# Gathers of edge rows without a wait between them, one wait at the end of each pass

## The chip, the cores and the metric

The kernel runs on one core of a Trainium2 chip. TensorE (PE, its weight loads PEld), VectorE (DVE), ScalarE (ACT), GpSimd (POOL) and SyncE (SP) each run their own instruction stream and meet at semaphores; DMAs are issued by SP and POOL (a few by ACT) and run on 16 DMA engines. The metric is the device time of one execution in microseconds, the median of several.

## The reference

A graph of 50000 nodes with 128 float32 features each and 25000 edges sorted by their target passes through four networks, one after the other; after each one the input is added and a layer norm follows. The first, a graph attention network of four layers, is the one that the change touches:

```
def _gat_layer(x, src, dst, ea, W, We, a_s, a_d, a_e, b, g, beta):
    h = x @ W
    e = ea @ We
    alpha = h @ a_s
    alpha = alpha[src] + (h @ a_d)[dst] + e @ a_e
    alpha = leaky_relu(alpha); alpha = _segment_softmax(alpha, dst, N)
    out = segment_sum(h[src] * alpha[:, None], dst) + b
    return layer_norm(out) * g + beta
...
for l in range(L):                      # L = 4, self loops added to the edges
    x = _gat_layer(x, src_f, dst_f, ea_f, W[l], ...)
```

`h[src]`, one row of 128 features and its attention term for every edge, is what the changed lines fetch. The other three networks (a relation network, a graph convolution, a convolution with edge weights) are outside the change.

## The kernel before, in words

The edges are laid out in K = 196 columns of 128: edge p of column c sits in partition p. The nodes are worked in 98 blocks of 512 rows. Nodes without an edge into them ("plain") need no neighbours, so the kernel works them through the layers on their own; nodes with edges live in "slots".

The attention network is a chain of passes. Each is a `Pass` whose five instruction streams start together and meet at its end in a barrier (L76); then POOL clears the pass's semaphores and a second barrier (L79) lets the next pass start. For each layer l there are three: p0 to p3 bring the edges' rows of layer l into the SBUF tile `H` (128 partitions x 196 columns x 136 floats) and do other work beside it; `soft(l)` computes the attention weights from `H`; `slots(l)` sums the weighted rows and writes layer l + 1's table.

What runs beside the gathers differs. In p0 it is `PlainLayers`: all 98 blocks of plain nodes go through the first layers, loaded and stored by SP, with TensorE, ScalarE and VectorE in a written order; at the end of its loop DVE and PE compute the logit terms (`Logits`, 1027 to 1036 us of the profile). In p0 POOL first gathers 196 columns of target rows (L2406) for the slots, which SP stores, and only then the source rows. In p1 to p3, `plain_rows` runs `Plain`: 32 or 33 blocks each of the plain nodes' way through the second and third networks; per block SP issues two loads, the stores of `n0`, of three tables of rows (L2667) and of `z` (L2672). At its end SP waits until all of these have landed (L1599).

The gathers are `gather_rows`, called by `FirstRows.gpsimd` (p0) and `Rows.gpsimd` (p1 to p3). POOL issues one indirect DMA a column (L2358): 128 rows, 544 bytes each in p0 and 528 after it, picked by an index tile, each with the semaphore `got[c % RING]`, RING = 16. Every 16 columns POOL waits until all 16 semaphores have reached the count of the rounds so far (L2355 to L2357), and after the last column for all of them once more (L2360, L2361). In p0 there is another wait before column 164, since `H`'s last 32 columns first hold the slot rows that SP stores. No instruction of the pass reads the source rows; the first to do so is `soft(l)`.

Gathers in other passes have no such ring: L1695 (`rel_rows`, `n_rows`) and L1909 (`sage_rows`) wait only until a buffer of four columns, of which there are four, has been consumed.

Of the kernel before, what the change touches and what calls it, by code (L numbers as in the profile page):

```python
# [32 lines left out]
RING = 16  # L33
# [2314 lines left out]
def gather_rows(kn, pool, got, table, index, rows, width, before=()):  # L2348

    K, bound = kn.K, pool.to_reg(rows - 1)  # L2350
    for c in range(K):
        if c == K - 8 * KT:
            for s, n in before:
                pool.wait_ge(s, n)
        if c and c % RING == 0:  # L2355
            for j in range(RING):
                pool.wait_ge(got[j], c // RING * 16)  # L2357
        pool.indirect_dma_start(kn.H[:, c, 0:width], None, table, bass.IndirectOffsetOnAxis(index[:, c:c + 1], 0),  # L2358
                                bounds_check=bound, oob_is_err=False).then_inc(got[c % RING], 16)
    for j in range(RING):  # L2360
        pool.wait_ge(got[j], len(range(j, K, RING)) * 16)  # L2361


class FirstRows(Stream):
# [31 lines left out]
    def gpsimd(self, pool):  # L2396
        kn = self.kn
        last_row = pool.to_reg(kn.NP - 1)
        for g in range(kn.KG):
            if g >= 4:  # L2400
                pool.wait_ge(self.dput[g % 4], g // 4 * 16)
                pool.wait_ge(self.heads_kept, g - 3)
                pool.wait_ge(self.attr_kept, g - 3)
            for k in range(KT):
                c = g * KT + k
                pool.indirect_dma_start(self.dg[:, g % 4, k, :], None, kn.t0w, bass.IndirectOffsetOnAxis(kn.dst_i[:, c:c + 1], 0),  # L2406
                                        bounds_check=last_row, oob_is_err=False).then_inc(self.dgot[g % 4], 16)
        gather_rows(kn, pool, self.got, kn.t0w.rearrange("n (q w) -> (n q) w", q=2), kn.src2_i, 2 * kn.NP, T0W, self.ends())
# [17 lines left out]
class Rows(Stream):  # L2426
# [11 lines left out]
    def gpsimd(self, pool):  # L2438
        kn = self.kn
        gather_rows(kn, pool, self.got, kn.tab[self.l], kn.idx, kn.NP + kn.ND, TW)  # L2440
# [671 lines left out]
```

## Time and profile before

| what | value |
|---|---|
| timed runs | 5356.57, 5367.84, 5373.27 us; median 5367.84 |
| profiled execution, first to last instruction | 5398.9 us |
| busy PE, PEld, DVE, ACT, POOL | 71%, 58%, 70%, 59%, 54% |
| p0, first gather of L2358 to the next pass | 772.7 to 1085.9 us |
| p1 | 1281.4 to 1597.6 us |
| p2 | 1793.3 to 2111.1 us |
| p3 | 2305.3 to 2621.1 us |

The page has no other time of the profiled execution than this span. The shares of busy time are means over a chain of passes with different limits, so the passes are read one by one. A wait is put down to the event that came last by the profile; at a barrier that is an engine's sequencer (a name with a q, as POOLq or PEq), and which engine was the late one has to be read from the timeline. DMA share is the busy share of the 16 DMA engines over all queues, summed over packets that may overlap, so it can pass 1. Part 5 of the page and the waits name a group by line and engine; POOL's gathers show as DMA_INDIRECT, their length being the time of the instruction on POOL and not of the transfer.

### The profile page before, as it was taken

The numbers are of one execution on the slowest core, as the hardware profiler recorded it, in microseconds if no ns is written. First come the engines' busy times: TensorE is split into PE (matmuls) and PEld (weight loads), VectorE is DVE, ScalarE is ACT, GpSimd is POOL, SyncE is SP. The second block draws the span as 40 slices with busy tenths as digits, with TensorE's granted clock in tenths as the row PEclk, the third lists the DMA queues.
The fourth block names the chain that finished last, engine by engine and source line by source line (L and its number), as shares of the span: only waits on it lengthen the run. The fifth ranks groups of instructions, "written<-read, shape, count | busy, mean of one in ns | idle before, by whom it ended". The sixth has DMA issues, their size and how long they took to land. (4 is left out here: it accounts for less than half of the span.)

```text
span 5398.9 us, 104328 instructions
## 1 busy us (share of the span) xinstructions
PE 3821.1 (71%) x23663; PEld 3143.4 (58%) x23663; DVE 3792.3 (70%) x10843; ACT 3176.1 (59%) x11279; POOL 2893.9 (54%) x2759
## 2 busy tenths in 40 slices
PE   6355889566747685768575768678688787977775
PEld 5354778565537453645474545456577676866665
DVE  2575889688849784978596767677567675756666
ACT  2022889577848684868482323356577685655554
POOL 0466766603650463066205867676376564757776
PEclk8698999888979797979676767677799998988777
DMA  8898999556955694578463446555489797872221
GB/s 183 129 301 269 383 362 278 176 148 179 283 175 149 203 283 154 156 229 278 149 184 126 131 129 189 167 158 177 165 282 303 248 305 238 246 189 66 62 66 57
DMA packets 918273, 1074.23 MB, mean 199 GB/s; under 512 B 202780, under 2 KB 565066, under 8 KB 917107
## 3 DMA queue, kind: packets, MB, share of 16 engines
q1 hardware_dynamic: 763570, 890.24, 50.5%
q0 software_dynamic: 90944, 180.06, 13.6%
q10 hardware_dynamic: 63556, 1.81, 1.6%
q8 instruction: 56, 0.92, 0.1%
q14 instruction: 147, 1.20, 0.1%
HBM read 509.54 MB, written 566.14 MB: 199 GB/s over the span
## 5 line engine op out<-in xcount | busy, mean ns | idle before, releaser
L2358 POOL DMA_INDIRECT H<-gat_rows,src_i x784 | 804.1, 1026 | 1032.9 <-POOLq L79 620.9
L1909 POOL DMA_INDIRECT s_G<-sage_rows,src_i x588 | 602.4, 1025 | 369.6 <-issue 161.0
L1695 POOL DMA_INDIRECT r_G<-rel_rows,idx x392 | 441.7, 1127 | 216.8 <-issue 110.2
L1708 PE MATMUL r_t<-r_oh,relv 8*128 8x512 f32 x294 | 227.4, 862 | 217.5 <-issue 77.2
L2547 PE MATMUL p_M<-Wg,p_hT 128*128 128x132 f32 x2352 | 336.6, 287 | 63.1 <-DVE p_res L2604 48.8
L1743 ACT ACTIVATE r_mT<-r_t 128x512 f32<-128x512 f32 x147 | 87.4, 594 | 460.4 <-PE r_t L1711 460.1
L2547 PEld LDWEIGHTS p_M<-Wg,p_hT 128*128 128x128 f32 x2352 | 290.3, 192 | 113.0 <-issue 96.0
L2604 DVE SCALAR_TENSOR_TENSOR p_res<-p_M,p_rr,cg 128x132 f32<-128x132 f32 x1176 | 333.8, 346 | 2.5 <-PE p_M L2547 1.4
L1304 PE MATMUL d_S<-ones,d_sqT 128*128 128x1 f32 x1568 | 224.3, 264 | 144.0 <-DVE d_ve L1449 144.0
L2686 PEld LDWEIGHTS p_pl_p<-Wn,p_pl_h 128*128 128x128 f32 x1568 | 205.9, 198 | 201.8 <-ACT p_pl_h L2780 154.9
L2686 PE MATMUL p_pl_p<-Wn,p_pl_h 128*128 128x128 f32 x1568 | 225.3, 289 | 132.6 <-ACT p_pl_h L2780 132.4
L1304 PEld LDWEIGHTS d_S<-ones,d_sqT 128*128 128x128 f32 x1568 | 217.0, 214 | 172.2 <-issue 133.4
L1605 DVE TENSOR_TENSOR_SCAN r_agT<-same_run,r_agT,r_mT 128x512 f32<-128x512 f32 (+1 forms) x144 | 184.4, 1281 | 185.2 <-ACT r_mT L1743 185.1
L1711 PEld LDWEIGHTS r_t<-share_squares,r_G 128*128 128x128 f32 x1176 | 200.8, 258 | 160.5 <-issue 160.5
L963 POOL DMA_INDIRECT gat_rows<-early_mapv,early_mput x196 | 195.1, 995 | 168.8 <-DMA gat_rows<-early_self_map 57.6
L1695 POOL DMA_INDIRECT r_G<-n_rows,src_i x196 | 235.4, 1201 | 78.5 <-issue 54.2
L2119 POOL DMA_INDIRECT share_squares<-features,src_i x196 | 217.1, 1108 | 94.6 <-issue 58.6
L1353 ACT ACTIVATE d_hs<-d_hs,pl 128x128 f32<-128x128 f32 x784 | 248.4, 399 | 15.8 <-DMA d_hs<-gat_rows 11.9
L2406 POOL DMA_INDIRECT H<-gat_rows,dst_i x196 | 196.1, 1001 | 92.9 <-issue 48.9
L1443 DVE TENSOR_TENSOR_SCAN d_yT<-same_run,d_yT,d_T 128x512 f32<-128x512 f32 (+1 forms) x192 | 244.5, 1273 | 0.3 <-ACT d_sqT L1359 0.2
L2111 POOL DMA_INDIRECT out_dram<-tp_v,put_i x196 | 198.7, 1014 | 77.6 <-issue 56.7
L1711 PE MATMUL r_t<-share_squares,r_G 128*128 (+1 forms) x1176 | 236.6, 363 | 0.0
(482 smaller groups left out, 12286.0 us busy)
## 6 DMA issues: line engine op xcount, KB each, us to landing
gat_rows<-p_res SPq DMA_DIRECT2D x294, 264.0 KB
sage_rows<-p_pl_s SPq DMA_DIRECT2D x294, 256.0 KB
gat_rows<-x_row SPq DMA_DIRECT2D x98, 536.0 KB
gat_rows<-d_res SPq DMA_DIRECT2D x147, 264.0 KB
d_hs<-gat_rows SPq DMA_DIRECT2D x147, 256.0 KB
s_hT<-sage_slots_t SPq DMA_DIRECT2D x147, 256.0 KB
slot_rows<-H SPq DMA_DIRECT2D x49, 544.0 KB, 11.5
x_x<-in_x SPq DMA_DIRECT2D x98, 256.0 KB
```

What stands on the lines that cost most here:

```text
L1304: mm = pe.matmul(pS[:, k:k + 1], sqT[:, b.s2, k * P:(k + 1) * P], self.ones[:, :], start=True, stop=True)
L1353: last = act.activation(hs[:, b.s4, k, :], hs[:, b.s4, k, :], ACT.Copy, scale=self.pl[:, bass.ds(b.n * KT + k, 1)])
L1443: v.tensor_tensor_scan(yT[:, b.s4, :], self.same[:, bass.ds(b.n * BLOCK, BLOCK)], pT[b.s2][:, :], 0.0 if first else yT[:, (b.m - 1) % 4, B ...
L1695: pool.indirect_dma_start(self.G[:, g % 4, k, :], None, table, bass.IndirectOffsetOnAxis(index[:, c:c + 1], 0), bounds_check=bound, oob_is ...
L1708: pe.matmul(pt[:, :], kn.relv[:, l, :], self.oh[:, b.m % self.Y, :], start=True, stop=False)
L1711: mm = pe.matmul(pt[:, k * P:(k + 1) * P], self.G[:, b.s4, k, :], share, start=False, stop=(k == KT - 1))
L1909: pool.indirect_dma_start(self.G[:, g % 4, k, :], None, kn.st[self.l], bass.IndirectOffsetOnAxis(kn.idx[:, c:c + 1], 0), bounds_check=boun ...
L2119: pool.indirect_dma_start(self.G[:, c, :], None, kn.f, bass.IndirectOffsetOnAxis(kn.idx[:, c:c + 1], 0), bounds_check=bound, oob_is_err=Fa ...
L2358: pool.indirect_dma_start(kn.H[:, c, 0:width], None, table, bass.IndirectOffsetOnAxis(index[:, c:c + 1], 0), bounds_check=bound, oob_is_er ...
L2547: mm = pe.matmul(self.pM[self.bank(b, j)][:, k // 2, (k % 2) * TW:(k % 2 + 1) * TW], self.hT[l][:, b.s2, k * P:(k + 1) * P], kn.Wg[:, l, : ...
L2604: last = v.scalar_tensor_tensor(self.res[l][:, b.s4, k, :], self.pM[self.bank(b, j)][:, k // 2, (k % 2) * TW:(k % 2 + 1) * TW], self.rr[l] ...
L2686: mm = pe.matmul(bank[:, k * D:(k + 1) * D], xT[:, k * P:(k + 1) * P], w, start=True, stop=True)
```

## The change

The wait inside the loop goes; the one after the loop stays. The semaphores are counted up as before, 12 or 13 gathers to each.

```
--- before.py
+++ after.py
@@ -2352,9 +2352,6 @@
         if c == K - 8 * KT:
             for s, n in before:
                 pool.wait_ge(s, n)
-        if c and c % RING == 0:
-            for j in range(RING):
-                pool.wait_ge(got[j], c // RING * 16)
         pool.indirect_dma_start(kn.H[:, c, 0:width], None, table, bass.IndirectOffsetOnAxis(index[:, c:c + 1], 0),
                                 bounds_check=bound, oob_is_err=False).then_inc(got[c % RING], 16)
     for j in range(RING):
```

## Rows read from the trace of the kernel before

**Rows 1.** Page, part 5: busy us, mean ns, idle us before.

```profile
L2358 POOL DMA_INDIRECT H<-gat_rows,src_i x784 | 804.1, 1026 | 1032.9 <-POOLq L79 620.9
L1909 POOL DMA_INDIRECT s_G<-sage_rows,src_i x588 | 602.4, 1025 | 369.6 <-issue 161.0
L1695 POOL DMA_INDIRECT r_G<-n_rows,src_i x196 | 235.4, 1201 | 78.5 <-issue 54.2
```

**Rows 2.** POOL's waits in p0, p1, p2, p3: total us, times, longest us.

```profile
POOL H L2358 <- DMA H<-gat_rows,src_i: 52.9, 28, 5.5
...
POOL H L2358 <- DMA H<-gat_rows,src_i: 49.2, 27, 4.7
...
POOL H L2358 <- DMA H<-gat_rows,src_i: 50.6, 24, 5.3
...
POOL H L2358 <- DMA H<-gat_rows,src_i: 45.3, 19, 4.9
```

**Rows 3.** SP's waits at the ends of p0 to p3, same columns.

```profile
SPq L76 <- PEq L76: 55.0, 1, 55.0
...
SPq L76 <- PEq L76: 39.6, 1, 39.6
...
SPq L76 <- PEq L76: 32.0, 1, 32.0
...
SPq L76 <- PEq L76: 30.9, 1, 30.9
```

**Rows 4.** DVE's waits, 1000 to 1086 us, same columns.

```profile
DVE soft_pen L1174 <- PEq L79: 49.7, 1, 49.7
```

**Rows 5.** Timeline of p0 and p1: start us, length us, [idle before].

```profile
772.66 1.00 POOL L2358 DMA_INDIRECT H<-gat_rows,src_i  x1 [0.30 <-issue]
...
1069.05 0.99 POOL L2358 DMA_INDIRECT H<-gat_rows,src_i  x1 [2.37 <-DMA H<-gat_rows,src_i]
1070.35 1.00 POOL L2358 DMA_INDIRECT H<-gat_rows,src_i  x1 [0.30 <-issue]
1072.95 1.00 POOL L2358 DMA_INDIRECT H<-gat_rows,src_i  x1 [0.30 <-issue]
1085.92 0.33 SPq L1167 DMA_DIRECT2D same_run<-same_as_before  x1
...
1281.44 1.00 POOL L2358 DMA_INDIRECT H<-gat_rows,src_i  x1 [207.48 <-POOLq L79]
...
1584.92 1.00 POOL L2358 DMA_INDIRECT H<-gat_rows,src_i  x1 [0.30 <-issue]
1597.62 0.33 SPq L1167 DMA_DIRECT2D same_run<-same_as_before  x1
```

**Rows 6.** Windows in p0: length, busy us, then clock, DMA share, GB/s.

```profile
700.00:800.00 100.00, 82.91 (x630) 73.00 (x629) 85.29 (x299) 80.12 (x307) 65.99 (x66) 0.98 1.03 364
800.00:1000.00 200.00, 195.68 (x1559) 176.35 (x1557) 199.58 (x737) 186.89 (x694) 126.90 (x127) 1.00 0.92 281
1050.00:1065.00 15.00, 0.00 (x0) 0.00 (x0) 0.00 (x0) 0.00 (x0) 11.62 (x12) 0.50 0.24 55
```

**Rows 7.** Windows' sums in p1 to p3: 18 bursts, then 21 pauses.

```profile
sum 387.90, PE 315.20 PEld 224.98 DVE 333.36 ACT 326.35 POOL 300.54; mean PE 17.51 PEld 12.50 DVE 18.52 ACT 18.13 POOL 16.70
...
sum 90.80, PE 66.18 PEld 48.87 DVE 72.80 ACT 79.04 POOL 0.39; mean PE 3.15 PEld 2.33 DVE 3.47 ACT 3.76 POOL 0.02
```

**Rows 8.** Windows of L2358 alone, from SP's end in p1, p2, p3.

```profile
1557.00:1586.00 29.00, 19.98 (x20) 0.50 0.20 45
2078.00:2100.00 22.00, 14.95 (x15) 0.50 0.21 46
2589.00:2610.00 21.00, 14.05 (x15) 0.50 0.20 45
```

**Rows 9.** One line's view, L2358: from issue to landing.

```profile
DMA to landing us min/median/max: 2.5/4.0/5.9
```

**Rows 10.** Window of the third sage_rows pass, columns as in rows 6.

```profile
4541.90:4801.40 259.50, 236.87 (x1698) 202.74 (x1699) 176.82 (x399) 161.86 (x481) 200.09 (x196) 0.95 0.76 233
```

More of the change, by code:

```diff
@@ L2354, in gather_rows @@
                 pool.wait_ge(s, n)
-        if c and c % RING == 0:
-            for j in range(RING):
-                pool.wait_ge(got[j], c // RING * 16)
         pool.indirect_dma_start(kn.H[:, c, 0:width], None, table, bass.IndirectOffsetOnAxis(index[:, c:c + 1], 0),
```

## The prediction

> **What bounds the kernel now.** I read the costliest groups of instructions first, because the change touches one line of them. The gathers into `H` (L2358) are 784 instructions, 196 in each of four passes p0 to p3, 1.03 us each; POOL is busy 804 us with them and idle 1033 us before them [rows 1]. Of that idle time 620.9 us lies before the first gather of p1, p2 and p3, while other passes run, and is no loss. The reader should split the rest by what ended it, which the waits of POOL, pass by pass, do: 52.9, 49.2, 50.6 and 45.3 us ended by the landing of these same gathers [rows 2]. That is the ring wait: after 16 issues POOL waits for all 16 semaphores, the one of the gather just issued too, so it drains what is in flight.
>
> POOL's idle time matters only where POOL ends the pass. The barrier waits at the pass ends show that: SP has everything stored and then waits 55.0, 39.6, 32.0 and 30.9 us [rows 3]. The profile puts this down to a "PEq" because all engines meet there; the timeline names the late one. In p0, DVE's last instruction is long over (its next one follows 49.7 us of idle time [rows 4]), while POOL still gathers at 1072.95 and the next stage starts at 1085.92; in p1, 1584.92 and 1597.62 [rows 5]. From the start of POOL's last gather to the next stage it is 12.97 and 12.70 us, the same tail twice. So each of the four passes ends with POOL alone, and what it saves there is saved in the span, until the next engine is the last. The chain that ended last reaches back only into the final pass, so it says nothing here.
>
> **The change part by part.**
>
> Removed: the waits at c = 16, 32, ..., 192, twelve rounds in each pass. A gather that waits for nothing follows the one before by 1.00 us of work and 0.30 us of idle time [rows 5], so each of the counted waits has 0.30 us that stays. What goes is 52.9 - 28 x 0.30 = 44.5 us in p0, 49.2 - 27 x 0.30 = 41.1 in p1, 50.6 - 24 x 0.30 = 43.4 in p2 and 45.3 - 19 x 0.30 = 39.6 in p3 [rows 2]. The 0.30 us before each of the other gathers, put down to "issue", stays.
>
> Left and moved: the final wait for all 16 semaphores and the 12.7 to 13.0 us tail behind the last gather come earlier by the same amount. Nothing on POOL is queued behind the removed waits but the gathers themselves. In p0 the gathers of the last 32 columns still wait for the slot rows' stores; the slot rows were all gathered before the first of these gathers, so that wait has 164 gathers, some 214 us, of room.
>
> Next late. In p0, POOL's tail would begin 44.5 us earlier, so the next stage would start at 1085.92 - 44.5 = 1041.4. DVE was free 49.7 us before its next instruction, that is at 1036.3 [rows 4]; even with some 1.2 us for the barrier it is ready for a start at 1037.5. POOL stays the last by 4 us and p0 saves all 44.5. In p1, SP waited 39.6 us and POOL saves 41.1: SP, with its stores, is now the last, and 39.6 is saved. In p2 SP allows 32.0 of POOL's 43.4, in p3 30.9 of 39.6 [rows 2, 3]. The sum is 44.5 + 39.6 + 32.0 + 30.9 = 147.0 us. Some 20 us of POOL's gain in p1 to p3 (1.5 + 11.4 + 8.7) are worth nothing, because there SP's stores end the pass.
>
> What the denser gathers cost the others. Alone, gathers at the unwaited pace take a DMA share of 0.24 (1050 to 1065 us), and with the layers' transfers the share is 0.92 (800 to 1000) [rows 6]. In that 200 us window POOL ran the gathers at 127/200 of full busy time against 11.62/15 alone [rows 6], so without waits the share would rise by 0.24 x (0.775/0.635 - 1) = 0.05, to 0.97. Before the change the same pace already stands in the trace: within a burst of 16, nothing waits. So the best row for the cost is a comparison of bursts and pauses. In p0, DVE is busy 199.58 of 200 us over bursts and pauses alike [rows 6]: the layers don't notice. In p1 to p3, summed over 18 bursts and 21 pauses, DVE is busy 333.36 of 387.9 us in bursts (86%) and 72.80 of 90.8 in pauses (80%), PE 81% and 73%, ACT 84% and 87% [rows 7]. No engine of the plain rows gets slower while gathers run, so the lower end is 0. The upper end is the DMA time of the gathers that fall into other work now: 20, 15 and 15 of them ran after SP had finished [rows 8], and 50 x 1.305 us x 0.24 share = 15.7 us, if DMA time were all that counted. The nearest row is the burst and pause comparison, which says none; as DVE does wait for the `z` rows' stores in these passes, I take a third, 5 us.
>
> The forecast is 147 - 5 = 142 us: 5398.9 - 142 = 5257 in the profiled execution. The profile gives no other time of that execution than its span, and the timed runs have their median 31 us (0.6%) below it; the removed idle time should be the same in both, so 5367.8 - 142 = 5226 us, 2.6% less.
>
> **Does the queue fill?** The waits also keep at most 16 gathers in flight, so what stands in their place if they go must be priced. A gather landed 2.5 to 5.9 us after its issue, 4.0 in the median [rows 9]; at 1.305 us a gather that is 2 to 5 in flight, far from 16. And the third pass over `sage_rows` (L1909) issues 196 gathers without such a wait: 259.5 us from first to last, 1.33 us each, at a DMA share of 0.76 [rows 10]. p0 to p3 would take 195 x 1.305 = 254 us and a little more.
>
> The Trainium skill speaks against the change at one place: "DMA: Bandwidth & Descriptors", section "Queues, rings and completion order", has each DMA engine take turns between the queues that have work, a packet at a time. By that rule gathers that never pause would take turns from SP's loads and stores all the time, not in 4 of 5 parts of it, and the third rival below would be the outcome; by the bursts of this trace they take the turns already and nobody waits longer. I go by the rows.
>
> **The rivals.**
>
> *Gathers slow down (12%).* Each gather costs more when nothing pauses it. For it: the gathers of `n_rows` (L1695), also without ring waits, took 1201 ns on average [rows 1], 1.50 us with the 0.30. Against it: the bursts' own 1.00 us and rows 10. At 1.50 us a pass would take 195 x 1.50 = 292.5 us. Against the gathers of p0, 300.3 us from first to last, and of p1, 303.5 [rows 5], this saves 7.8 and 11.0; about 11 in p2 and p3 as well. That makes 41 us, POOL still last everywhere: 5327.
>
> *The transfers of p1 to p3 get late by their share (8%).* The 15.7 us are paid in full and the layers of p0 lose as much as a pass does, 5 us. Saved: 147 - 21 = 126, so 5242.
>
> *DMA saturates and the pass itself gets longer: slower than before (3%).* Between 700 and 800 us, with other gathers and their stores, the share was 1.03 and DVE got through 85.29 of 100 us against 99.8 later [rows 6], a factor of 1.17. If gathers without pauses drive the passes there, the 264 us of p0 from the first gather to DVE's end grow by 45 and eat its 44.5; the some 275 to 285 us of p1 to p3 grow by 47 to 48 each and SP's 39.6, 32.0 and 30.9 are overrun by 7, 16 and 17. In sum 40 us more: 5408. It decides from a slowing by 14% in p1 and 11% in p2 and p3; the 0.97 worked out above speaks against it.
>
> *The waits were not what held the gathers (3%).* If the engine stops by itself where the wait stood, for room in its queue, all stays: 5368. Against it: rows 10, where 196 follow one another with no such stop.
>
> **How the numbers follow.** The forecast gets 74%, 5226 with its own range of 5208 to 5245 (147 saved with 12 of luck and the spread of the timed runs, 5357 to 5373, to 125 saved). The range of 8 in 10 goes up past the second rival and partly to the first: 5205 to 5275. A measurement of this kernel tells 0.3% (16 us) from no change; all cases but the last two are faster by more. Faster 0.94, same 0.03, slower 0.03.
>
> **What would show it.** In the changed trace, the waits of POOL on its own gathers should be gone from L2358 but for a few of 0.3 us; 196 gathers should take 254 to 265 us from first to last; SP's wait at the barrier should be near 10 us in p0 (POOL last) and next to nothing in p1 to p3, while POOL arrives there a little early. The start of the stage behind p0 should move to about 1041 us. The forecast is wrong if the mean of a gather grows beyond 1.1 us, if landing takes 10 us or more, or if the last store of SP in p1 comes later than 276 us after its first gather by more than 5 us.

## The result, and the profile after

| | before | changed |
|---|---|---|
| timed runs, median (range) | 5366.06 us (5356.57 to 5373.27) | 5225.52 us (5209.77 to 5228.46) |
| profiled execution | 5398.9 us | 5208.0 us |

Ratio 0.9726, 95% interval 0.9705 to 0.9746: 140.5 us less, faster clear of noise. The forecast was 5226 us.

The costliest groups of the changed kernel, the two that fill `H` (L2355 was L2358, L2403 was L2406), to be read beside [rows 1]:

```profile
L2355 POOL DMA_INDIRECT H<-gat_rows,src_i x784 | 799.4, 1020 | 867.7 <-POOLq L79 629.7
L2403 POOL DMA_INDIRECT H<-gat_rows,dst_i x196 | 195.5, 997 | 91.9 <-issue 58.5
```

The work on POOL is the same, 1.02 us a gather; the idle time before the gathers fell by 165 us, from 1032.9 to 867.7, and of what is left 629.7 is again the time between the passes. What ended the rest: POOL's waits on its own landings, over the whole execution,

```profile
POOL H L2355 <- DMA H<-gat_rows,src_i: 0.9, 3, 0.3
```

and, in p0, p1, p2 and p3, on nothing that the profile shows:

```profile
POOL H L2355 <- issue: 59.1, 194, 0.3
...
POOL H L2355 <- issue: 59.1, 194, 0.3
...
POOL H L2355 <- issue: 59.4, 195, 0.3
...
POOL H L2355 <- issue: 59.1, 194, 0.3
```

Where [rows 2] had 28, 27, 24 and 19 waits on landings, each pass now has 195 gaps of 0.3 us, and no gap is longer than that. The next view is the timeline, the starts and ends of p0 and p1, as in [rows 5]:

```profile
758.36 1.00 POOL L2355 DMA_INDIRECT H<-gat_rows,src_i  x1 [0.30 <-issue]
...
1012.06 1.00 POOL L2355 DMA_INDIRECT H<-gat_rows,src_i  x1 [0.30 <-issue]
...
1024.76 0.33 SPq L1167 DMA_DIRECT2D same_run<-same_as_before  x1
...
1219.53 0.99 POOL L2355 DMA_INDIRECT H<-gat_rows,src_i  x1 [206.47 <-POOLq L79]
...
1478.78 0.99 POOL L2355 DMA_INDIRECT H<-gat_rows,src_i  x1 [0.30 <-issue]
...
1487.38 0.93 SPq L2669 DMA_DIRECT2D plain_z_t<-p_pl_zT  x2
1493.11 0.33 SPq L1167 DMA_DIRECT2D same_run<-same_as_before  x1
```

From first to last, p0's 196 gathers take 253.7 us (300.3 before), p1's 259.3 (303.5). From the last gather of p0 to the next stage it is 12.70 us (12.97 before); in p1 it is 14.33, since POOL's wait for its last landings took 1.6 us longer there (last section). SP's waits at the four barriers say by how much, in the order of [rows 3]:

```profile
SPq L76 <- PEq L76: 7.5, 1, 7.5
...
SPq L76 <- PEq L76: 1.3, 1, 1.3
...
SPq L76 <- PEq L76: 0.2, 1, 0.2
...
SPq L76 <- PEq L76: 0.2, 1, 0.2
```

55.0, 39.6, 32.0 and 30.9 us have become 7.5, 1.3, 0.2 and 0.2. DVE in p0, as in [rows 4], was idle 49.7 us and now is

```profile
DVE soft_pen L1174 <- PEq L79: 2.5, 1, 2.5
```

In p2 and p3 SP, whose stores land last, now ends the pass; in p0 and p1 POOL still does, by 1.3 us or so. From the first gather to the next stage the four passes got shorter by 46.9, 42.6, 36.6 and 30.1 us (313.3, 316.2, 317.8 and 315.8 before; 266.4, 273.6, 281.1 and 285.7 now).

Those are 156 us, and the two profiled executions differ by 191. The other 35 lie in stages that the change doesn't touch (first gather of p0 at 772.66 before, 758.36 now, for one). The profiled execution of before was longer than any of its timed runs (5373.27), so it is the wrong base by some 30 us, and that of the changed kernel is the fastest of its four (5209.77); the timed runs carry the result, and the experiments below give a better base for the passes.

### The profile page after: what moved, and what is told of

Same layout as the page of the kernel before. It is cut to its first block and busy times, and to the rows that moved or that the text cites. A ratio compares the mean times of both kernels' runs of the same rounds, so it can differ in the third digit from the quotient of the medians.

```text
span 5208.0 us, 103944 instructions
## 1 busy us (share of the span) xinstructions
PE 3805.0 (73%) x23663; PEld 3130.7 (60%) x23663; DVE 3790.4 (73%) x10843; ACT 3173.8 (61%) x11279; POOL 2875.7 (55%) x2759
## 5 line engine op out<-in xcount | busy, mean ns | idle before, releaser
L2355 POOL DMA_INDIRECT H<-gat_rows,src_i x784 | 799.4, 1020 | 867.7 <-POOLq L79 629.7
L2403 POOL DMA_INDIRECT H<-gat_rows,dst_i x196 | 195.5, 997 | 91.9 <-issue 58.5
```

## The experiments

"Passes" below are p0 to p3 from their first gather to the next stage.

**Is it the drain, or the wait as such?** The old wait drains the queue: POOL stands still until all that it has issued has landed. From the kernel before, with a lagged wait instead, for the gather issued 16 earlier:

```
-        if c and c % RING == 0:
-            for j in range(RING):
-                pool.wait_ge(got[j], c // RING * 16)
+        if c >= 16:
+            pool.wait_ge(got[(c - 16) % RING], ((c - 16) // RING + 1) * 16)
```

> Starts from the kernel before. POOL still holds at most 16 gathers in flight, but before gather c it waits only for gather c - 16, 16 issues earlier, not for all issued so far. Theory (the cost of the old wait was the drain: the gather that POOL waited for had been issued 1.3 us before and lands 2.5 to 5.9 us after its issue): gather c - 16 was issued 16 x 1.305 = 20.9 us earlier and has landed, so nothing is waited for; 196 gathers in 254 to 261 us, waits on their own landing near 0, time as the changed kernel, 5226 within 16 us. Rival (the gain comes from having no wait instructions at all, or from more than 16 gathers in flight): at least half of the 141 us are lost, 5295 or more.

Measured: 5220.1 us (ratio to the kernel before 0.9741, 95% interval 0.9711 to 0.9771; ratios below come with the same interval), passes 266.4, 273.7, 285.3 and 281.7 us, 1107.0 in sum beside 1106.8 of the changed kernel. POOL's waits over the execution:

```profile
POOL H L2357 <- issue: 236.5, 776, 0.3
POOL H L2357 <- DMA H<-gat_rows,src_i: 1.5, 5, 0.3
```

With 180 waits a pass, 720 in all, and never more than 16 gathers in flight the gain is all there. What cost the time was that the round's last gather, issued one gather earlier, had to land before the next one was issued. The trace of the kernel before shows it directly: in each of the 36 rounds of p1 to p3 the next gather starts 0.79 to 0.81 us after the landing of the round's last one. The rival is out.

**Do the passes add up?** The ring wait is kept where `before` is empty, that is in p1 to p3:

```
-        if c and c % RING == 0:
+        if not before and c and c % RING == 0:
```

> The change made in p0 alone; p1 to p3 keep their waits. Theory (each pass ends with POOL and the passes add up): p0 gets shorter by 45 to 47 us, p1 to p3 stay at 316 to 318 us, time 5366 - 46 = 5320. Rival (DMA backlog in p0 is handed on, or the gain is one of the whole program and not of a pass): p0's gain is under 30 us or p1 changes as well.

Measured: 5318.1 us (0.9919, 0.9892 to 0.9945), 50 us less than the kernel before beside it (5368.0). Passes 267.4, 313.9, 313.0 and 313.5. SP's waits at the four barriers:

```profile
SPq L76 <- PEq L76: 9.9, 1, 9.9
...
SPq L76 <- PEq L76: 42.2, 1, 42.2
...
SPq L76 <- PEq L76: 30.5, 1, 30.5
...
SPq L76 <- PEq L76: 34.2, 1, 34.2
```

p0 has its 46 us, the other three are as before and SP waits there as in [rows 3]. This execution is also the better base for p1 to p3: with waits 940.4 us, without (changed kernel) 840.4. So p1 to p3 give 100.0 us and p0 46, together 146, where the first two profiles side by side said 156.

**Who holds whom after the change?** The changed kernel without the gathers of every second column in p1 to p3:

```
+        if not before and c % 2:
+            continue
         pool.indirect_dma_start(kn.H[:, c, 0:width], None, table, ...
...
-    for j in range(RING):
+    for j in range(0, RING, 1 if before else 2):
```

> The changed kernel, with the gathers of every second column of p1, p2 and p3 left out (3 x 98 of 588; their columns of H keep the rows of the layer before, and the output is not the reference's). Theory (after the change SP with the stores of the plain rows ends p2 and p3, in p1 POOL is the last by 1 us only, and the gathers' DMAs hold nobody up): POOL is done 127 us earlier in each pass and the time moves by 1 to 6 us, 5221. Rival (gathers without pauses slow the plain rows through the DMA engines): 294 x 1.305 us x 0.24 = 92 us of DMA time are gone; if a third of it counted, 5195, if all, 5134.

Measured: 5206.1 us (5189.1 to 5217.2), 14 to 19 us under the changed kernel's medians of two occasions (5225.5, and 5219.6 below). The passes p1 to p3 take 271.2, 279.9 and 279.5 us, 9.8 less in sum than in the changed kernel. (Six executions whose gathers are all there and never stop, two of the changed kernel, one with the lag of 16 and three with `place_in_map` changed, below, have sums of 836.8 to 843.5, so this difference is good to some 3 us.) SP's waits there:

```profile
SPq L76 <- PEq L76: 0.2, 1, 0.2
...
SPq L76 <- PEq L76: 0.2, 1, 0.2
...
SPq L76 <- PEq L76: 0.2, 1, 0.2
```

SP is the last in all three, with POOL done 129 us after its first gather. So POOL no longer sets the passes: half its gathers gone buys 1 us in p1 and, through SP, some 9 us more, 6 to 13 in all by that scatter. I had expected 1 to 6 in all, and the timed median moved by more than the passes do. Of 92 us of DMA time left out, about a tenth comes back; a third (5195 us) lies within the spread of its timed runs but not in its passes.

**The same edit where there is little slack.** Slack is what the next engine leaves: how much earlier POOL may be done before another one ends the pass. `place_in_map` has the same ring. The changed kernel without it:

```
         for c in range(first, end):
-            if c and c % RING == 0:
-                for j in range(RING):
-                    pool.wait_ge(self.placed[j], c // RING * 16)
             pool.indirect_dma_start(pieces, ...
```

> The changed kernel with the same edit made to place_in_map (L963), which scatters 196 columns with the same ring of 16 before p0. Its waits on its own landings add up to 49 us in 20 times, 43 us over the 0.3 us that stay. Theory (a wait is worth only what the next engine leaves): in the pass of the first scatters SP waits 18.9 us at the barrier for POOL and one round of some 1.6 us goes; in the pass of the others SP waits only 5 to 8 us for POOL, so 5 to 8 us of the 41 are saved: together 7 to 10, 5217. Rival (the sum of the removed waits is saved, as it nearly was in p0 to p3): 5226 - 43 = 5183.

Measured: 5195.3 us (5187.7 to 5217.5) in four runs. In the second of the two passes the changed kernel has, first POOL's waits on its own scatters, then SP's wait for POOL:

```profile
POOL gat_rows L963 <- DMA gat_rows<-early_mapv,early_mput: 46.7, 18, 6.0
```

```profile
SPq L76 <- PEq L76: 8.0, 1, 8.0
```

and without the ring, over the execution and then for POOL's idle time between its last scatter and p0:

```profile
POOL gat_rows L960 <- DMA gat_rows<-early_mapv,early_mput: 0.3, 1, 0.3
...
POOL H L2400 <- POOLq L79: 47.5, 1, 47.5
```

46.7 us of waits were there to remove and POOL now sits idle 47.5 us at the end; the pass got shorter by 6.4 us (275.7 to 269.3, from barrier to barrier), the pass before it by 3.9, where 1.6 was expected. As the timed runs scattered more than these 10 us, the two kernels were timed again, side by side:

> The changed kernel once more, as the base for the other two on the same chip: 5224 within 8 us.

> The changed kernel with place_in_map without its ring waits too, timed again beside the changed kernel: its passes said 8 to 10 us, its four timed runs 25 to 30. Theory (slack): 7 to 12 us under the changed kernel, 5214. Rival (sum of the waits): 40 us under it, 5184.

Measured: 5219.6 (5212.4 to 5230.4) and 5211.0 us (5204.2 to 5215.2): 8.6 us. The ranges still overlap a little; in the two profiles of this occasion the two passes together got shorter by 10.5 us. The slack, not the sum of the waits, is what the edit is worth, and of the 24 to 30 us between the first medians all but these 9 were scatter.

**What does a round cost?** The kernel before with a drain every 8 gathers:

```
-        if c and c % RING == 0:
-            for j in range(RING):
-                pool.wait_ge(got[j], c // RING * 16)
+        if c and c % 8 == 0:
+            for j in range(min(c, RING)):
+                pool.wait_ge(got[j], len(range(j, c, RING)) * 16)
```

> The kernel before with the same drain after every 8 gathers in gather_rows instead of every 16: 24 rounds a pass in place of 12. Theory (a round costs one landing, whatever its length: 44.5, 41.1, 43.4 and 39.6 us for 12 rounds, 3.3 to 3.7 us each): as much again, p0 to p3 longer than before by 168 us in all, 5366 + 168 = 5534. Rival (what counts is how many gathers are in flight on average, which halving the round hardly changes from 3): under 60 us more.

Measured: 5520.9 us (1.0287, 1.0257 to 1.0317), 152 us more than before. A round of p1 in the timeline:

```profile
1394.52 0.99 POOL L2358 DMA_INDIRECT H<-gat_rows,src_i  x1 [3.20 <-DMA H<-gat_rows,src_i]
...
1404.27 1.03 POOL L2358 DMA_INDIRECT H<-gat_rows,src_i  x1 [0.30 <-issue]
1411.37 0.99 POOL L2358 DMA_INDIRECT H<-gat_rows,src_i  x1 [6.07 <-issue]
```

Eight gathers, then 6.07 us of idle time. First to last it is 346.0, 338.6, 339.9 and 339.7 us, 152 us more than before in sum, and SP's waits grew to

```profile
SPq L76 <- PEq L76: 100.8, 1, 100.8
...
SPq L76 <- PEq L76: 80.8, 1, 80.8
...
SPq L76 <- PEq L76: 77.0, 1, 77.0
...
SPq L76 <- PEq L76: 70.7, 1, 70.7
```

The 48 rounds added cost 152 us, 3.2 us each, somewhat less than the first 48, which had cost 178.7 from first to last gather (3.7 each; 168.6 by the counted waits alone). Every microsecond of it shows in the time, since POOL is the last in all four passes. The rival is out.

**How deep must the queue be?** As the first experiment with 4, and with 2, in place of 16:

```
-        if c >= 16:
-            pool.wait_ge(got[(c - 16) % RING], ((c - 16) // RING + 1) * 16)
+        if c >= 4:
+            pool.wait_ge(got[(c - 4) % RING], ((c - 4) // RING + 1) * 16)
```

> Before gather c POOL waits for gather c - 4 alone. Theory (a gather lands 2.2 to 5.9 us after its issue, at 1.305 us a gather; four issues take 5.2 us): only the slowest landings are waited for, mostly in p0, under 5 us a pass; 5226 within 20 us. Rival (a deep queue is needed to keep the DMA engines at the gathers): a pass of 196 gathers takes 280 us or more.

> Before gather c POOL waits for gather c - 2 alone. Theory: two gathers take as long as one landing, 3.1 us and some 0.2 us of waiting in p1 to p3 (1.6 us a gather, 315 to 325 us for 196) and 3.5 to 4 us in p0 (1.9 us a gather, 340 to 390 us); POOL ends every pass again, as late as before or later: 5400 to 5470. Rival (with two in flight the landing gets so short that the issue still sets the pace): 196 gathers in under 275 us, 5226 to 5250.

Measured with 4: 5240.2 us (0.9764, 0.9736 to 0.9792), first to last 267.9, 268.1, 265.5 and 267.5 us, with these waits on landings in all:

```profile
POOL H L2357 <- DMA H<-gat_rows,src_i: 60.3, 114, 1.6
```

That is 15 to 20 us of the gain lost, of which p0 has 14, more than the 5 a pass expected there: 24.2 of these 60.3 us stand in p0. (The 2.2 us of the expectation should be 2.5, the shortest landing in these traces.) With 2: 5584.5 us (1.0405, 1.0366 to 1.0445), slower than before, first to last 367.3, 349.7, 349.5 and 350.4. In p1:

```profile
1402.83 1.00 POOL L2357 DMA_INDIRECT H<-gat_rows,src_i  x1 [2.59 <-DMA H<-gat_rows,src_i]
1404.13 1.00 POOL L2357 DMA_INDIRECT H<-gat_rows,src_i  x1 [0.30 <-issue]
1407.18 1.00 POOL L2357 DMA_INDIRECT H<-gat_rows,src_i  x1 [2.05 <-DMA H<-gat_rows,src_i]
1408.48 1.00 POOL L2357 DMA_INDIRECT H<-gat_rows,src_i  x1 [0.30 <-issue]
1410.96 1.14 POOL L2357 DMA_INDIRECT H<-gat_rows,src_i  x1 [1.48 <-DMA H<-gat_rows,src_i]
```

```profile
DMA to landing us min/median/max: 2.5/3.1/5.7
```

Gathers go in pairs, each pair a landing behind the one before. I had put 3.3 us on a pair in p1 to p3, 3.1 for the landing and 0.2 of waiting, and got 2 x 349.7/195 = 3.59. The trace has both parts: in p1 the recorded landings (74 of 196) take 3.23 us in the mean, and a gather starts 0.34 us in the mean after the landing that it waits for. The direction was right, the size, 5400 to 5470, was not. Between 2 and 16 in flight lies all of the effect, and 4 is nearly enough.

**A version that beats both.** The last two passes before p0 share the scatters: `EARLY` says how many columns go into the first. Since the second now has POOL idle, 16 of them are moved:

```
-    EARLY = 24
+    EARLY = 8
```

> As the one before, and EARLY from 24 to 8: 16 of the 24 scatters of the first of these two passes go into the second, where POOL is now done 36 us before SP. Theory (slack): 16 x 1.277 = 20.4 us go from POOL in the first pass, where SP leaves 16; the second takes them for nothing (36 - 20 = 16 us left). 16 us under the one before, 5198. Rival (the second pass gets longer, by the scatters' place or their DMAs beside its loads): 0 to 5 us under it.

Measured: 5198.3 us (ratio to the kernel before 0.9689, 0.9667 to 0.9711), 12.7 under the one before and 21.3 under the changed kernel. In the first pass SP's wait for POOL, then POOL's idle time behind the second:

```profile
SPq L76 <- PEq L76: 0.2, 1, 0.2
...
POOL H L2400 <- POOLq L79: 29.9, 1, 29.9
```

The first pass lost 16.6 us (84.3 to 67.7), as the slack said; the second, in which SP is the last and POOL has room, grew by 4.2 (268.8 to 273.0). 16 scatters more beside its loads and stores are not free; whether that is their place in time or their DMAs was not tried.

## Why the prediction was right, point by point

*The path.* That POOL alone ends the four passes, and that the time beyond the next engine is worth nothing, carried the forecast. The same edit was worth 46 us in p0, where 44.5 us of waits met 49.7 of slack, and some 9 us in `place_in_map`, where 46.7 us of waits stood in a pass in which SP left 8.0.

*The waits.* 44.5, 41.1, 43.4 and 39.6 us were to go. First to last, the gathers got shorter by 46.6, 44.2, 45.3 and 42.6, some 2 to 3 us a pass more: one gap of 1.6 to 1.9 us in each pass that stood under "issue" (behind column 112) went as well, and the gathers themselves got 4 to 8 ns shorter each. In p0 that adds to the saving; in p2 and p3, which SP ends, it is worth nothing.

*Who is late next.* p0: POOL by 4 us, measured 1.3 (DVE's 2.5 less the 1.2 for the barrier); p2 and p3: SP, as said. p1 was called for SP by 1.5 us and went to POOL by 1: SP came 4 us earlier than in the profile of before, and POOL's tail, which the prediction took as fixed at 12.7 us, was 14.33. In the second profile of the changed kernel SP is the last there. Nothing hangs on it.

*The denser gathers.* Term 5 us, bounds 0 and 15.7. SP arrives at its barrier 830.8 us after the first gathers of p1 to p3 (sum) in the kernel of the second experiment, with waits there, 836.0 without, 827.4 with half the gathers. That reads as 5 us for the pauses and 9 for half the gathers, but from one execution each: the five other executions whose gathers never stop give 833.0 to 839.7, and the profile of the kernel before, a long execution, 844.5 with waits. So the runs bound the term at some 9 us and don't show that it is 5. The busy shares of [rows 7] could not tell it either: they say how long an engine works, not how late its data comes. In p0, over the 200 us that answer to those of [rows 6],

```profile
784.00:984.00 200.00, 195.69 (x1559) 176.35 (x1558) 199.60 (x736) 186.52 (x690) 153.07 (x155) 1.00 0.95 289
```

DVE is busy 199.60 of 200 again, at a DMA share of 0.95 (0.97 worked out) and with POOL at 153 for 127. The third of the upper bound that I took was a choice; nothing here contradicts it.

*The Trainium skill's rule* of engines that take turns between queues ("DMA: Bandwidth & Descriptors", "Queues, rings and completion order") would, as the prediction reads it, have made SP's transfers pay for gathers that never pause. By the arrivals above they pay between nothing and 9 us of some 840: if they take turns, it costs little at this pace of issue. The turns themselves no run here shows.

*The rivals.* A slower gather: 1.02 us, not 1.2. A full queue: no stop in 196. Saturation: the share stayed below 1 in the stretch above. The DMA engines were not what paced the gathers in these four passes; POOL's own 1.30 to 1.34 us a gather was.

*The landing times.* The prediction read the 2.5 to 5.9 us of [rows 9] as what a gather takes. The trace has the landings of only 72 of the 784 gathers, the last two of each round in p1 to p3, and the changed kernel's trace has none. Its conclusion, 2 to 5 in flight, fits the lagged runs all the same: 4 in flight lost 15 to 20 us, 16 nothing.

*The base.* The sum was made against 5398.9, and 5257 was forecast for the profiled execution; 5208 came. The rest is no effect of the change: the profiled execution of before lay 32.8 us above the median of its timed runs, that of the changed kernel 17.5 below its own. Carrying the saving over to the median in microseconds was right.

*The half microsecond.* 5226 against 5225.5 is closer than the terms were known, and that is luck: the second median of the changed kernel was 5219.6, SP's waits of 39.6, 32.0 and 30.9 us were 42.2, 30.5 and 34.2 in another execution, and the 5 us were chosen.

## What to carry to other kernels

A ring of semaphores should wait for the slot that is about to be reused, not for all of the ring: the same 16 in flight cost 141 us when drained and nothing when lagged. How many to keep in flight follows from the trace, landing time over issue period, here 2.5 to 5.9 us over 1.3, that is 2 to 5; measured, 4 were nearly enough and 2 far too few. Before removing a wait, read what the next engine waits at the same barrier: the removal is worth the smaller of that number and the sum of the waits.

## What the runs showed that was not expected

Where POOL is the last, 12.7 us lie between the start of its last gather and the next stage, in p0 with no rounds as in p1 with rounds of 16 and of 8 (1649.51 to 1662.21). The trace of the changed kernel tells what they are: POOL's instructions at the barrier, at the end of p0, begin with

```profile
L76 POOLq DRAIN  x2: 34/4046/8057, 1015.6 to 1024.7; - x2
```

that is, POOL's wait for the last landings is over 3.4 us after the start of the last gather, then one DRAIN instruction of 8.06 us runs from 1015.6 to 1023.7, and 1.1 us later the next stage starts (the other DRAIN in the line, 34 ns long, comes behind the barrier). In p1 the first part takes 5.0 us, hence the 14.33. The DRAIN takes 8.05 or 8.06 us at the end of p0 to p3 in every run here, with half the gathers too, where it comes some 130 us before the barrier; at the ends of other passes POOL's DRAIN takes up to 26 us. Where POOL ends the pass, these 8 us are part of the time; what sets their length, and whether they can be moved or shortened, was not tried.

A drain every 8 gathers showed idle times of 6.07 us under "issue", which the profile elsewhere uses for time with no visible cause. The program has POOL wait for its gathers there, so the likely reason is a landing that was not recorded.
